# Reordered loads and weight composition ahead of a two-layer transformer kernel, and a new table of steps in its first layer

## The reference, cut to what matters

```python
# layer 0 attention, per head: everything ahead of the scores is linear but the RMS norm
q_c = xh @ W_DQ.T @ W_UQ.T;  q = [rms(q_c), rms(q_c) @ W_QR.T]
k_c = xh @ W_DKV.T @ W_UKV_k.T;  k = [rms(k_c), xh @ W_KR.T]
attn = softmax(q @ k.T * scale + causal);  out = (attn @ v_c) @ W_O.T
# layer 0 feed-forward: r = sigmoid(xr @ W_r.T); out = r * (relu(xk @ W_k.T)**2 @ W_v.T)
# layer 1 attention: the same shape, no causal mask, a bias by position
# layer 1 feed-forward: gelu(x @ W1) @ W2 with weights that are composed once:
W = einsum('k,kir,kro->io', softmax(logits), A, B)     # 32 primitives of rank 64, for W1 and for W2
```

## Time and profile before

| | |
|---|---|
| median of 3 runs | 1679.16 us (1672.22 to 1690.13) |
| the profiled execution, its own time | 1679.12 us |
| its span (first to last instruction) | 1677.4 us |
| body 0 of layer 0 can start (first exponential) | 109.26 us |
| one body of layer 0 | 42.1 us |
| data moved in the first fortieth of the span (42 us) | 292 GB/s |

### The profile page before, as it was taken

How to read it: one execution, slowest core, us unless ns; L and a number is a source line. 1 busy time by engine, 2 the same in 40 slices (tenths; PEclk the granted TensorE clock), 3 DMA queues, 4 the chain that set the end, 5 groups by cost and what they waited for, 6 DMA issues and landing times.

```text
span 1677.4 us, 42102 instructions
## 1 busy us (share of the span) xinstructions
PE 1495.5 (89%) x16234; PEld 605.6 (36%) x16234; DVE 1342.3 (80%) x2493; ACT 1251.7 (75%) x2502; POOL 1037.8 (62%) x1369
## 2 busy tenths in 40 slices
PE   3879999999999899988899999999999999999995
PEld 1644444444444444433223323232323323232331
DVE  2177777777777777788898898989988988889880
ACT  1237777777777777765788888888888888888884
POOL 2346777777777777744656656566566656665565
PEclk9879999999999999999999999999999999999998
DMA  9322222222232322222322222222322233222200
GB/s 292 59 60 69 83 75 80 77 79 75 67 91 62 86 73 83 73 71 63 60 67 53 62 54 69 58 53 59 64 68 53 48 67 74 56 55 49 68 15 19
DMA packets 133159, 116.96 MB, mean 70 GB/s; under 512 B 16856, under 2 KB 125664, under 8 KB 132960
## 3 DMA queue, kind: packets, MB, share of 16 engines
q1 hardware_dynamic: 126272, 100.64, 24.5%
q0 software_dynamic: 4096, 8.40, 1.5%
q10 hardware_dynamic: 2592, 5.24, 0.9%
HBM read 79.63 MB, written 33.55 MB: 67 GB/s over the span
## 4 chain that ended last, share of the span: by engine, by line
PE 51%; DVE 15%; ACT 14%; POOL 10%; issue 5%; DMA 3%; SPq 2%; DVEq 0%; POOLq 0%; ACTq 0%
PE pv_acc L656 14%; PE scores_transposed L672 12%; PE scores_transposed L594 11%; ACT probs L979 8%; PE scores_for_max L693 4%; POOL turn L1285 4%; DVE maxs L1189 3%; PE scores_for_max L594 3%; DVE maxs L1192 2%; DMA stacks<-parts_scratch 2%; PE scores_transposed L765 2%; DVE maxs L1216 2%; POOL rrms L1285 1%; PE scores_for_max L722 1%; DVE ssq L1131 1%
## 5 line engine op out<-in xcount | busy, mean ns | idle before, releaser
L979 ACT ACTIVATE probs<-scores_transposed 128x512 f32<-128x512 f32 x1664 | 909.1, 600 | 153.7 <-PE scores_transposed L672 143.6
L672 PE MATMUL scores_transposed<-stacks 62*128 62x512 bf16 (+3 forms) x2048 | 576.6, 344 | 45.5 <-ACT probs L979 23.7
L1374 POOL TENSOR_TENSOR probs<-probs,near_bias 128x512 f32<-128x512 f32 x256 | 333.2, 1304 | 315.9 <-ACT probs L979 314.7
L656 PE MATMUL pv_acc<-probs,vals 128*32 128x512 f32 (+3 forms) x4096 | 464.4, 525 | 7.4 <-POOL probs L1348 7.4
L1189 DVE TENSOR_REDUCE maxs<-scores_for_max 128x2 f32<-128x1024 f32 x325 | 390.5, 1220 | 70.5 <-PE scores_for_max L693 68.6
L672 PEld LDWEIGHTS scores_transposed<-stacks 62*128 62x128 bf16 x2048 | 158.7, 94 | 609.0 <-ACT probs L979 278.6
L693 PE MATMUL scores_for_max<-stacks 60*128 60x512 bf16 x1024 | 329.8, 385 | 10.3 <-DVE maxs L1189 7.6
L1192 DVE TENSOR_REDUCE maxs<-scores_for_max 128x1 f32<-128x512 f32 x374 | 245.3, 682 | 13.3 <-PE scores_for_max L693 11.6
L697 PE MATMUL scores_for_max<-stacks 60*128 60x512 bf16 (+3 forms) x1024 | 237.5, 307 | 9.4 <-DVE maxs L1220 3.5
L1220 DVE TENSOR_REDUCE maxs<-scores_for_max 128x1 f32<-128x512 f32 x256 | 175.1, 684 | 85.7 <-PE scores_for_max L709 85.2
L1348 POOL TENSOR_SCALAR_AFFINE_SELECT probs<-probs 128x512 f32<-128x512 f32 x256 | 160.8, 641 | 46.7 <-ACT probs L979 46.1
(11 more groups left out here) (135 smaller groups left out, 2010.0 us busy)
## 6 DMA issues: line engine op xcount, KB each, us to landing
stacks<-parts_scratch SPq DMA_DIRECT2D x768, 64.0 KB
parts_scratch<-parts SPq DMA_DIRECT2D x64, 384.0 KB, 2.6
x_tile<-in_L_attn_x_dram SPq DMA_DIRECT2D x16, 256.0 KB, 2.9
probs<-in_fc_B_dram ACTq DMA_DIRECT2D x1, 4096.0 KB, 21.5
stage_a<-in_fc_A_T_dram SPq DMA_DIRECT2D x1, 4096.0 KB, 16.4
stacks<-mT SPq DMA_DIRECT2D x256, 4.0 KB
x_res<-in_L_attn_x_dram SPq DMA_DIRECT2D x16, 256.0 KB, 3.5
x_tile<-x_between_layers SPq DMA_DIRECT2D x16, 256.0 KB, 2.8
```

The costliest lines, as they stand in the source:

```text
L656: last = mm(acc[VW * j:VW * j + VW, q0:T], columns[:, first:first + VW], probs[:, row, column:column + width], start=(kt == 0 and pu % PAI ...
L672: last = mm(st[:, bank, column:column + T - q0], ks[p][rows, h, P * kt:P * kt + P], qs[p][rows, h, q0:T], start=True, stop=True)
L979: fn(probs[:, row, :], st[:, B.use(("st", u, number)).bank, :], ACT.Exp, scale=SCALE).then_inc(s["exp_done"], 1)
L1374: g.tensor_tensor(diag, diag, near_bias[:, kt, :].unsqueeze(1).broadcast_to([P, G, P]), ALU.mult).then_inc(s["emul_pool"], 1)
```

## The change

It has two halves. The first is in the set-up and the first two bodies:

- The 18 small loads are split between SyncE and ScalarE, nine each, and stand first on both queues. SyncE then issues all big loads, in the order fc1_A, fc1_B in two halves, fc2_A, fc2_B, and after them the ten later loads.
- `set_up` on VectorE finishes `wcat` before the logits' softmax instead of after it. ScalarE's exponentials wait for a step that now comes later (`setup_dve` 5).
- The 16 products of W1 no longer stand at every second slot from 24 but eleven at slots 30 to 40 and five at 56 to 60. The 64 products of W2 are spread over the whole second body: 26 up to slot 13, then three in four slots.
- The stacks of sequence 0 are loaded by two queues: SyncE issues the 12 DMAs of the queries, ScalarE the 12 of the keys (ahead of its second body).
- fc1_A is staged in `vals` and fc2_B in `probs`, so the clearing of `vals` can stand before the second body, on GpSimd. `weigh(1)` follows the copy of W1 on VectorE instead of preceding it.

```diff
-COMPOSE_FROM = 24
-COMPOSE_SECOND = [min(2 * slot, NF * NC) for slot in range(NG * NT * G + 1)]
+COMPOSE_FROM = ((30, 0, 11), (56, 11, NC))
+COMPOSE_SECOND = [min(2 * slot, 26 + 3 * max(slot - 13, 0) // 4, NF * NC) for slot in range(NG * NT * G + 1)]
...
-        stage_a1 = probs[:, NC:2 * PACK_ROWS].rearrange("p a n -> p (a n)")
-        stage_b2 = vals[:, 1].rearrange("p a b n -> p (a b n)")
+        stage_a1 = vals[:, 1].rearrange("p a b n -> p (a b n)")
+        stage_b2 = probs[:, NC:2 * PACK_ROWS].rearrange("p a n -> p (a n)")
...
+        def load_setup(eng, which):
+            for dst, src in setup_loads[which::2]:
+                eng.dma_start(dst, src).then_inc(setup_in, 16)
...
             first = body(Body(0, FIRST))
             next(first)
-            for dst, src in loads:
-                sp.dma_start(dst, src).then_inc(setup_in, 16)
+            load_setup(sp, 0)
+            load_for_compose(sp, 0)
+            load_for_compose(sp, 1, 0, NC // 2)
+            load_for_compose(sp, 1, NC // 2, NC, 4)
+            load_for_compose(sp, 2)
+            load_for_compose(sp, 3)
             for dst, src in later_loads:
                 sp.dma_start(dst, src).then_inc(later_in, 16)
-            load_for_compose(sp, 3)
-            sp.wait_ge(compose_in[1], 16)
-            load_for_compose(sp, 2)
             run(first)
...
-            load_for_compose(act, 0)
-            load_for_compose(act, 1)
-            act.wait_ge(setup_dve, 4)
+            load_setup(act, 1)
+            act.wait_ge(setup_dve, 5)
...
             run(body(Body(0, FIRST)))
             act.wait_ge(setup_pool, 6)
+            act.wait_ge(S[0]["parts_stored"], 32)
+            for t, part in enumerate(K_PARTS):
+                heads = parts_dram[1, part].rearrange("(h e d) n -> e d h n", e=E, d=HD)
+                for e in range(E):
+                    row = HALF * e + HD * t
+                    act.dma_start(ks[0][row:row + HD, :, :], heads[e]).then_inc(S[0]["stack_loaded"], 16)
             run(body(Body(0, FIRST + 1)))
-            act.wait_ge(stage_free, 3)
+            act.wait_ge(stage_free, 2)
+            act.wait_ge(setup_pool, 8)
...
             def before_second_body():
-                weigh(1)
                 dve.wait_ge(setup_pe, 3)
                 v.tensor_copy(w1[:], acc[:]).then_inc(stage_free, 1)
+                weigh(1)
...
-                v.memset(vals[:, 1], 0.0).then_inc(rep_chain, 1)
-                dve.wait_ge(rep_chain, 6)
-                v.memset(vals[:, 1, :, :, HD:HD + 1].rearrange("p t h d -> p (t h) d"), 1.0
-                         ).then_inc(stage_free, 1)
...
+            pool.wait_ge(stage_free, 1)
+            g.memset(vals[:, 1], 0.0).then_inc(setup_pool, 1)
+            pool.wait_ge(setup_pool, 7)
+            g.memset(vals[:, 1, :, :, HD:HD + 1].rearrange("p t h d -> p (t h) d"), 1.0).then_inc(setup_pool, 1)
```

```diff
-    0: {"MT0": (2, 0, 0), "FR": (7, 0, 1), "FK": (8, 0, 1), "OA": (15, 1, -1), "MT1": (23, 0, 0),
+    0: {"MT0": (2, 0, 0), "FR": (3, 1, 1), "FK": (7, 0, 1), "OA": (15, 1, -1), "MT1": (20, 0, 0),
```

More of the change, by code:

```diff
@@ L133 @@
 OTHER_WORK = {
-    0: {"LN": (5, 2), "NORM": (14, 2), "VALUES": (17, 1), "POST": (23, -1), "STORE": (26, -1),
+    0: {"LN": (6, 2), "NORM": (13, 2), "VALUES": (15, 1), "POST": (24, -1), "STORE": (25, -1),
         "SQUARE": (32, 2), "MEAN": (34, 2), "ROOT": (42, 2), "SCALE_QK": (47, 2), "POW": (10, 2),
-        "SECOND_Q": (52, 2), "THIRD_Q": (52, 2), "SECOND_K": (57, 2), "THIRD_K": (60, 2), "KACT": (10, 1),
-        "SCALE_K": (49, 2)},
+        "SECOND_Q": (52, 2), "THIRD_Q": (58, 2), "SECOND_K": (57, 2), "THIRD_K": (62, 2), "KACT": (23, 1),
+        "SCALE_K": (50, 2)},
     1: {"LN": (0, 2), "NORM": (17, 2), "BESIDE": (23, -1), "STORE": (39, -1), "POW": (1, 2),
@@ L410, in build @@
         bias_in = sem("bias_in")
-        compose_in = [sem(f"compose_in{i}") for i in range(4)]
+        compose_in = [sem(f"compose_in{i}") for i in range(5)]
         setup_dve = sem("setup_dve")
@@ L448, in load_for_compose @@
             stage, name = compose_loads[n]
-            eng.dma_start(stage.rearrange("p (c n) -> p c n", c=NC),
-                          a[name].rearrange("(c p) n -> p c n", p=P)).then_inc(compose_in[n], 16)
+            eng.dma_start(stage.rearrange("p (c n) -> p c n", c=NC)[:, first:last],
+                          a[name].rearrange("(c p) n -> p c n", p=P)[:, first:last]
+                          ).then_inc(compose_in[n if landed is None else landed], 16)
+        setup_loads = [
+            (small[0:64, 0, :], a["L0_attn_W_DQ"]), (small[0:64, 1, :], a["W_UQ_T"]),
+            (small[:, 2, :], a["L0_attn_W_DKV"]), (small[:, 3, :], a["W_UKV_K_T"]),
+            (small[0:64, 4, :], a["L0_attn_W_KR"]), (small[0:64, 5, :], a["L0_attn_W_QR"]),
+            (ukv_v[:], a["L0_attn_W_UKV"][HD:2 * HD, :]), (small[0:HD, 6, :], a["W_O_T"]),
+            (ident[:], a["ident"]), (blocks[:], a["blocks"]),
+            (normw[:, 0, :], a["L0_attn_q_norm_w"].unsqueeze(0).broadcast_to([P, HD])),
+            (normw[:, 1, :], a["L0_attn_k_norm_w"].unsqueeze(0).broadcast_to([P, HD])),
+            (lall[:, 0, :], a["L1_ffn_fc1_logits"].unsqueeze(0).broadcast_to([P, PRIM])),
+            (lall[:, 1, :], a["L1_ffn_fc2_logits"].unsqueeze(0).broadcast_to([P, PRIM])),
+        ] + [
+            (halves[HALF * e:HALF * e + HALF, n, :, :],
+             a[name].rearrange("(half r) n -> r half n", half=2))
+            for n, name in enumerate(("ident", "causal")) for e in range(E)
+        ]
@@ L597, in compose_first @@
             def compose_first(slot):
-                c = (slot - COMPOSE_FROM) // 2
-                if slot < COMPOSE_FROM or slot % 2 or c >= NC:
+                c = next((at + slot - f for f, at, end in COMPOSE_FROM if f <= slot < f + end - at), NC)
+                if c == NC:
                     return
```

31 lines of the change are left out of this document (17 added, 14 removed), and 4 rows, old and new, of the table WORK_USES.

## The result

| | before | changed |
|---|---|---|
| median of 20 runs each | 1678.09 us (1671.55 to 1690.13) | 1702.41 us (1681.39 to 1715.44) |
| the profiled execution, its own time | 1679.12 | 1702.57 |
| first exponential of body 0 of layer 0 | 109.26 | 112.13 |
| one body of layer 0 in the steady part | 42.15 | 43.32 |

The ratio is 1.0116 (95% interval 1.0094 to 1.0137): the kernel became **slower by 1.2%**, where 1665 was forecast and 1679 was the upper end of the range. The medians are of all runs and the ratios leave out runs of a slower state (here the four above 1706), so that the ratio is smaller than the 1.0145 of the medians. The 20 runs fall in two groups, 8 from 1681 to 1695 and 12 from 1701 to 1715. The mean granted clock (the share of TensorE's full clock) is 0.982 to 0.987 in the first and 0.969 to 0.977 in the second. The profiled execution is one of the second group.

A forecast was written before the change was run, and what follows sets the result against it. No single engine was taken to set the pace: a serial chain of waits bounds the set-up, and a chain over several engines each body. 1679.1 - 20.0 (first half) + 6.0 (table) = 1665.1 us; range 1650 to 1679.

The forecast's parts named there:

- Small loads: Set-up: the small loads, split over two queues, land at 9.3 instead of 23.02, -13.7 us.
- XT: Set-up: the exponentials wait for maxima taken behind `wcat`, so XT's step costs +2.9 us (0 to +3.5).
- Projection, QT to KT: Set-up: projection -4.2 and +0.6 us, QT to KT -1.0, third part of keys -1.3; parts stored at 44.8.
- Second body's start: TensorE starts the second body at 49.9 instead of 59.91, with the big loads done by then.
- To slot 32: Second body: the stacks no longer decide, so slot 32 is reached at 68.1 instead of 86.5, -18.4 us.
- The rule on queues: Stack loads: two queues share the same DMA engines, so stacks take 24.9 us again; by itself this gives 1667.
- Slots 32 to 63: Second body: 24 more products of W2 stand here and cost +0.8 us (-1.5 to +5.5).
- Body 0: Start of body 0: the clearing of `vals` now stands ahead of the second body, -2.4 us.
- A shorter chain is a shorter kernel, one for one: Everything up to body 0's first exponential: time saved there comes off the kernel in full.
- The table: Layer 0's bodies: new step order costs +0.4 us per body (-0.6 to +2.0), +6 in all.
- slower than before: Rival, chance 0.08: the `pv` stall at 36 is passed on in full, 2.0 us per body, giving 1693.
- The first half brings less: Rival, chance 0.15: slow W1 products, unhidden W2 products (4.7 us) or deciding stacks; one gives 1670, two 1675.

The follow-up runs named there:

- e4_clear_later: The changed kernel with GpSimd's clearing of `vals` and the stacks held back until VectorE's set-up copies are done; 1702.59 us (1.0128).
- e7_one_queue: The changed kernel with all 24 stack loads of sequence 0 issued by SyncE and none by ScalarE; 1693.83 us in a single run.
- e1_old_table: The changed kernel with layer 0's old table of steps, all of the first half kept; 1675.42 us (0.9977).
- e2_table_alone: The kernel before with only the new table of layer 0; 1695.3 us (1.008).
- e3_dense_w2: The changed kernel with the 64 products of W2 back in slots 0 to 31, two to a slot; 1694.55 us (1.0089).
- f1_mended_spread: The changed kernel with later clearing, stack loads all on SyncE, KACT, POST and STORE back at 10, 23, 26, W2's products still spread; 1682.44 us (1.0003).

## Why the prediction was wrong, step by step

The first exponential of body 0 was put at 89 and came at 112.13, which is 23.1 of the 37.3 us between forecast and median. What follows makes up the rest: 20.4 in the trace, put at 6, and 16.0 of it are the 1.17 per body of the table.

1. *Small loads* (-13.7): right. They landed at 10.36 instead of 9.3, -12.7.
2. *XT*: put at 18.5 with step 1, measured 24.26. Of the 5.8, 1.1 are step 1's landing. Not foreseen in any step: the 4.92 us copy beside the clearing. The clearing had stood at the same place before, but the copy came at 23.02, behind it. Moving the loads forward brought the two together. `e4_clear_later` shows it: XT at 19.65, 4.6 us earlier, and the first sum of squares 4.15 earlier. The Trainium skill ("GPSIMD Engine Reference", section "Specifications") has GpSimd's SBUF interfaces shared with VectorE, with contention for some of VectorE's modes; this trace agrees, with 4.92 against 0.29, though no run shows in which mode the copy ran.
3. *Projection, QT to KT* (3, 4): right in size. From XT to SCALE_QK's end it was 17.1 (24.26 to 41.37), put at 16.8 (18.5 to 35.3). From there to the parts stored it was 9.7, put at 9.5.
4. *Second body's start* (5): 54.70 against 49.9, late by what the copy cost. The big loads held nothing up.
5. *To slot 32* (6): the step failed in "I take that they no longer decide". The two queues brought no rate: 22.9 us from first issue to landing, against 24.9 with one queue and 15 at best in my sum. The rule on queues that the prediction weighed (the Trainium skill, "DMA: Bandwidth & Descriptors", section "Issuing engines are not separate DMA queues") was right: only issue time was saved, and `e7_one_queue` loses nothing without the second queue. By itself that error is small, since TensorE was ready at 72.33 and waited 1.73. Slots 0 to 31 took 17.6 us up to there, put at 18.2.
6. *Slots 32 to 63* (7, +0.8, "+5.5, if nothing hides them"): **the step that failed most**. The stretch grew by 17.0. I had the half clock in the earlier trace rows (0.62) and took it as a constant of the stretch, and in my upper bound priced each of the 24 moved products at the 0.23 of a dense row at full clock. Standing alone between other products one costs 0.42 at full clock and 0.72 at half: 24 at 0.72 are 17.3 where my bound was 5.5. Nor does anything hide them. With them, TensorE is what this stretch is made of: busy 21.30 of 22 at full clock (`e1_old_table`) and 36.56 of 37 at half. The right bounds were 22 and 37, not 18.2 and 25.2.
7. *Body 0* (8, -2.4): right in kind. The exponential follows W2's copy (110.69) by 1.4 instead of 3.1, so -1.7: the first transposed scores now start only behind that copy (111.41), and the exponential follows them.
8. *"A shorter chain is a shorter kernel, one for one"*: not so where the start did get shorter. In `e1_old_table` 12.0 us at body 0 became 6.3 of span.

**The table** (+0.4 per body): the mechanism was right and its size was not. The masks of slots 28 and 32 come late behind KACT, POST and the stores, as written, and `pv` waits at 36. Counted from the masks of 16 and 20, the mask of 28 was put 8.25 later and came 8.51 later; the root was put at 13.95 and came at 14.28. The idle time ahead of the root that I let "pay for half of it" is still there (0.42). With the masks themselves only 0.16 earlier in the body, and not 0.23, that is +0.9 at the root where I had +0.5. Behind the root I took 0.1 off for work that moves forward; instead 0.26 was added up to the next body. +1.17 is inside the bounds given (-0.6 to +2.0), and close to the 1.2 from which the rival *slower than before* was to decide. That rival's time of 1693 is near what `e2_table_alone` took (1695.3), but this is chance: the rival had the table cost 34 and the start bring 20, and in that kernel the table costs 16 and there is no new start. In the changed kernel the loss of the start's gain joined 1.17 per body.

**The rivals.** None of them had both, a start without gain and a table at three times its price. *The first half brings less* named the right two places (stacks that decide, products that are not hidden), but priced the second at 4.7, where it was 17.0. The range left both out.

## What to carry to other kernels

When work is moved from a stretch in which the bounding engine is waiting anyway to one in which it is nearly full, price the new stretch at both levels of TensorE's clock: slots 32 to 63 cost 19.4 us with dense products even with part of them at half clock, but 22 or 37 with spread ones. Price a product that stands alone by a row in which one does (0.42 here), not by a dense row (0.23). Before a load is made earlier, look for what runs on the neighbouring engine at its new time, and ask what will be waited for next: `e4_clear_later` gained 4.2 us of set-up, 1.4 of them were left at slot 32, behind the stacks, and 0.9 at body 0. Of a table of many numbers test single entries; three of them cost 1.4 us per body here, and the rest gained 0.2 to 0.3.

## What the runs showed of the hardware

- Once at 1.2 GHz, TensorE stayed there for about 40 us although it was busy for 36.56 of 37 us. It came back between 113 and 117, when the matmuls changed from single products between short maxima (161 in 37 us) to denser ones (77 in 4 us). The Trainium skill ("TensorE: Matmul & The Clock Gate", section "What's actually happening") says that activity releases the throttle; in this trace the engine was busy by the profile's count and the clock stayed low. What counts as activity no run here settles.
- A copy of 128x256 with conversion to bf16 on VectorE took 4.92 us (changed kernel) or 4.29 (`e1_old_table`) while GpSimd was clearing, and 0.29 otherwise. It ended with the clearing: in `e3_dense_w2` a first copy at 11.79, a second at 15.39, and two clearings at 11.65 and 15.24.
- The 24 stack loads of 64 KB took 20 to 25 us in the set-up, on one queue or on two, at a mean DMA share of 0.60 to 0.63 and 78 to 85 GB/s (changed kernel from 52 to 74, `e4_clear_later` from 49 to 72, `f1_mended_spread` from 50 to 73).
- A product of 128x128 by 128x128 in f32 took TensorE 0.23 us in a dense row, 0.42 alone between bf16 products of the maxima at full clock, and 0.72 there at half clock.
